# The second attention's scores and value products in fp32 instead of three fp32r products

## The reference, cut to what matters

```python
q = q * cos + _rotate_half(q) * sin          # 16 heads of 128, 256 tokens
kk = kk * cos + _rotate_half(kk) * sin       # 8 heads, each serves two query heads
att = jnp.einsum('shd,thd->hst', q, kk) / np.sqrt(HEAD_DIM)
att = jnp.where(causal[None], att, jnp.finfo(att.dtype).min)
att = jax.nn.softmax(att, axis=-1)
attn_out = jnp.einsum('hst,thd->shd', att, v).reshape(S, N_HEADS * HEAD_DIM) @ wo
x1 = x + attn_out
```

## Time and profile before

| | |
|---|---|
| median of 3 runs | 555.36 us (554.13 to 555.83) |
| profiled execution | 554.96 us |
| its span in the trace | 552.5 us |
| TensorE clock granted, mean | 0.976 of full speed |

### The profile page before, as it was taken

The page is one execution under the profiler, slowest core; times in us unless marked ns, Lnnn a source line. Parts: engine busy times, 40 slices in busy tenths (PEclk is TensorE's granted clock), DMA queues, the critical chain, the costliest instruction groups (busy, mean ns, idle before and its releaser), DMA issues. The chain is left out here.

```text
span 552.5 us, 11501 instructions
## 1 busy us (share of the span) xinstructions
PE 513.8 (93%) x4559; PEld 472.6 (86%) x4559; DVE 333.8 (60%) x647; ACT 256.0 (46%) x448; POOL 241.8 (44%) x207
## 2 busy tenths in 40 slices
PE   6978999999999999999998987889999799899984
PEld 6968899899999999989987976879988677799983
DVE  5977556763377887644437656899787545232331
ACT  8822233232256677422351426456767763554340
POOL 3022355242313432235257756544236124387983
PEclk9997999999999999999999988899999989999998
DMA  7813133202301011002405423545545632065522
GB/s 262 329 60 106 66 116 116 90 24 80 116 25 36 23 39 39 2 20 77 174 3 177 152 91 114 176 148 192 187 138 191 224 120 77 12 203 200 173 80 38
DMA packets 32884, 62.11 MB, mean 112 GB/s; under 512 B 3440, under 2 KB 3456, under 8 KB 32704
## 3 DMA queue, kind: packets, MB, share of 16 engines
q1 hardware_dynamic: 32288, 60.08, 32.5%
q0 software_dynamic: 544, 1.31, 1.2%
HBM read 48.27 MB, written 13.12 MB: 111 GB/s over the span
## 5 line engine op out<-in xcount | busy, mean ns | idle before, releaser
L1151 POOL TENSOR_TENSOR wlo<-raw,whi 128x512 fp32r<-128x512 f32 x96 | 129.7, 1383 | 106.3 <-ACT whi L525 106.2
L1215 PE MATMUL bank<-HTh,whi 128*128 128x256 f32 x224 | 64.6, 288 | 8.6 <-DVE rope L887 6.3
L1217 PE MATMUL bank<-HTh,wlo 128*128 128x256 f32 x224 | 64.1, 286 | 0.0
L1216 PE MATMUL bank<-HTl,whi 128*128 128x256 f32 x224 | 64.1, 286 | 0.0
L1132 POOL TENSOR_TENSOR state<-kv_new,state_dec 128x512 f32<-128x512 f32 x15 | 21.8, 1453 | 95.6 <-DVE kv_new L821 95.6
L810 DVE TENSOR_TENSOR A<-bank,DEC 128x512 f32<-128x512 f32 x64 | 39.7, 682 | 35.0 <-PE bank L1283 33.5
L525 ACT ACTIVATE whi<-raw 128x2048 fp32r<-128x2048 f32 x24 | 45.8, 1908 | 17.6 <-DMA raw<-in_w_down 12.5
L1215 PEld LDWEIGHTS bank<-HTh,whi 128*128 128x128 f32 x224 | 43.6, 195 | 10.0 <-issue 8.9
L1216 PEld LDWEIGHTS bank<-HTl,whi 128*128 128x128 f32 x224 | 43.6, 195 | 0.1
L1217 PEld LDWEIGHTS bank<-HTh,wlo 128*128 128x128 f32 x224 | 43.6, 195 | 0.0
L1261 PE MATMUL bank<-xTh,WKh 128*128 128x256 f32 x128 | 38.7, 303 | 2.3 <-DVE xTl L739 2.3
(11 more groups left out here) (283 smaller groups left out, 1560.1 us busy)
## 6 DMA issues: line engine op xcount, KB each, us to landing
X<-in_x SPq DMA_DIRECT2D x16, 256.0 KB, 3.4
xn_all<-XN SPq DMA_DIRECT2D x16, 256.0 KB, 2.8
uo_all<-uo SPq DMA_DIRECT2D x16, 256.0 KB, 2.7
raw<-in_wq SPq DMA_DIRECT2D x4, 1024.0 KB, 5.9
UR<-uo_all SPq DMA_DIRECT2D x16, 256.0 KB, 5.2
XR<-in_x SPq DMA_DIRECT2D x16, 256.0 KB, 3.0
out<-XR SPq DMA_DIRECT2D x16, 256.0 KB, 2.0
raw<-in_wo SPq DMA_DIRECT2D x4, 1024.0 KB, 5.9
```

The costliest lines, as they stand in the source:

```text
L1151: ins = Q.tensor_tensor(low[:, k, :], raw[b % 2][:, k, :], high[:, k, :].bitcast(f32), ALU.subtract)
L1215: T.matmul(dst, lh, rh, start=first, stop=False)
L1216: T.matmul(dst, lh, rl, start=False, stop=False)
L1217: return T.matmul(dst, ll, rh, start=False, stop=last)
```

## The change

The rotated queries and keys are written once, in fp32, straight into QR and KR by the sum that wrote `staged`. Values are copied once by ACT (VA). The transposed probabilities are copied once by ACT (PT). The low parts of queries, keys, values and probabilities are gone from DVE, and the high parts of queries and keys from ACT. The scores and the value product are one fp32 matmul each where there were three fp32r ones. The MLP's operand, which shared QRh and QRl, keeps its two parts under new names at the same addresses.

```diff
-        def unit_dst(u, part):
+        def unit_dst(u):
...
-                return (Vh, Vl)[part][i][:, p, :]
-            if k[0] == "Q":
-                return (QRh, QRl)[part][i][:, 2 * p:2 * p + 2, :].rearrange("p h m -> p (h m)")
-            return (KRh, KRl)[part][:, 4 * i + 2 * p:4 * i + 2 * p + 2, :].rearrange("p h m -> p (h m)")
+                return VA[i][:, p, :]
+            return QR[i][:, 2 * p:2 * p + 2, :] if k[0] == "Q" else KR[:, 4 * i + 2 * p:4 * i + 2 * p + 2, :]
...
-                    if u and units[u - 1][0][0] != "V":
-                        unit_high(u - 1)
-                    if units[u][0][0] == "V":
-                        unit_high(u)
+                elif u is not None and units[u][0][0] == "V":
+                    unit_values(u)
...
-                if h - 1 in unit_of_step:
-                    unit_high(unit_of_step[h - 1])
...
-                    S.activation(PTh[:, p % 2, :], B[4][:, 0:3 * P], ACT.Copy).then_inc(pt_hi, 1)
+                    S.activation(PT[:, p % 2, :], B[4][:, 0:3 * P], ACT.Copy).then_inc(pt_ok, 1)
...
-                if n >= 2:
-                    dve.wait_ge(unit_hi, before[-2] + 1), dve.wait_ge(unit_lo, before[-2] + 1)
...
-                V.tensor_tensor(staged[:, n % 2, :].rearrange("p (a m) -> p a m", a=2), rope1[:], rope2[:],
-                                ALU.add).then_inc(staged_ok, 1)
...
+                V.tensor_tensor(unit_dst(u), rope1[:], rope2[:], ALU.add).then_inc(rope_ok, 1)
...
-                if h - 1 in unit_of_step:
-                    unit_low(unit_of_step[h - 1])
...
-                if 0 <= p < FH:
-                    dve.wait_ge(pt_hi, p + 1)
-                    if p >= 2:
-                        dve.wait_ge(ot_ps, p - 1)
-                    low_of(PTl[:, p % 2, :], B[4][:, 0:3 * P], PTh[:, p % 2, :], pt_lo)
...
-                        pe.wait_ge(unit_lo, u + 1)
+                        pe.wait_ge(value_ok, value_count(u))
...
-                        ins = split_matmuls(B[h % 2][:, at:at + width],
-                                            (QRh[h // 4][:, h % 4, rows], QRl[h // 4][:, h % 4, rows]),
-                                            (KRh[:, kv, 0:width], KRl[:, kv, 0:width]), True, True)
+                        ins = T.matmul(B[h % 2][:, at:at + width], QR[h // 4][:, h % 4, rows], KR[:, kv, 0:width],
+                                       start=True, stop=True)
...
-                    pe.wait_ge(pn_ok, p + 1), pe.wait_ge(pt_lo, p), pe.wait_ge(ms_ok, N_TILES)
+                    pe.wait_ge(pn_ok, p + 1), pe.wait_ge(pt_ok, p), pe.wait_ge(ms_ok, N_TILES)
...
-                    split_matmuls(B[5][:, 0:SEL], (vh[:, 0, cols], vl[:, 0, cols]),
-                                  (PTh[:, g % 2, 0:SEL], PTl[:, g % 2, 0:SEL]), True, False)
-                    split_matmuls(B[5][:, P:SEL], (vh[:, 1, cols], vl[:, 1, cols]),
-                                  (PTh[:, g % 2, SEL:], PTl[:, g % 2, SEL:]), False, True).then_inc(ot_ps, 1)
+                    T.matmul(B[5][:, 0:SEL], VA[kv // 4][:, 0, cols], PT[:, g % 2, 0:SEL], start=True, stop=False)
+                    T.matmul(B[5][:, P:SEL], VA[kv // 4][:, 1, cols], PT[:, g % 2, SEL:], start=False, stop=True)\
+                        .then_inc(ot_ps, 1)
```

More of the change, by code:

```diff
@@ L59, in build @@
         xTh, xTl = (at(n, kb, [P, 2, NK, GROUP], f32r) for n, kb in (("xTh", 64), ("xTl", 72)))
-        KRh, KRl = (at(n, kb, [P, FKV, SEL], f32r) for n, kb in (("KRh", 64), ("KRl", 72)))
+        KR = at("KR", 64, [P, FKV, SEL])
         x1, delta = (at(n, kb, [P, NS, DM]) for n, kb in (("x1", 64), ("delta", 68)))
@@ L68, in build @@
         rope1, rope2 = (at(n, kb, [P, 2, SEL]) for n, kb in (("rope1", 88), ("rope2", 90)))
-        QRh, QRl = ([at(f"QR{i}{part}", kb, [P, 4, SEL], f32r) for i, kb in enumerate(homes)]
+        QR = [at(f"QR{i}", kb, [P, 4, SEL]) for i, kb in enumerate((112, 158, 96, 104))]
+        MTh, MTl = ([at(f"MT{i}{part}", kb, [P, 4, SEL], f32r) for i, kb in enumerate(homes)]
                     for part, homes in (("h", (112, 158, 96, 104)), ("l", (116, 162, 100, 108))))
         kh, kl, qh, ql = (at(n, 112 + 2 * i, [P, NK, P], f32r) for i, n in enumerate(("kh", "kl", "qh", "ql")))
-        Vh, Vl = ([at(f"V{i}{part}", kb, [P, NS, DM], f32r) for i, kb in enumerate(homes)]
-                  for part, homes in (("h", (92, 124)), ("l", (120, 128))))
+        VA = [at(f"VA{i}", kb, [P, NS, DM]) for i, kb in enumerate((92, 124))]
         X = at("X", 120, [P, NX, DM])
@@ L109, in build @@
         SM, PR, PN = (at(n, kb, [P, 2, 3 * P]) for n, kb in (("SM", 166), ("PR", 169), ("PN", 172)))
-        PTh, PTl = (at(n, kb, [P, 2, 3 * P], f32r) for n, kb in (("PTh", 175), ("PTl", 178)))
+        PT = at("PT", 175, [P, 2, 3 * P])
         OTh, OTl = (at(n, kb, [P, 2, SEL], f32r) for n, kb in (("OTh", 181), ("OTl", 183)))
@@ L204, in kq_count, with value_count @@
             return sum(units[n][0][0] != "V" for n in range(u + 1))
+        def value_count(u):
+            return u + 1 - kq_count(u)
         hi_after = {0: "Q2", 2: "O0", 4: "Q3", 6: "O1", 8: "O2", 9: "O3", 12: "G0", 16: "U0"}
@@ L282, in build @@
         cs_ok, ht_hi, ht_lo, sel_ok = sems("cs_ok ht_hi ht_lo sel_ok")
[L283 to L284 removed]
+        unit_ps, unit_b, rope_ok, value_ok = sems("unit_ps unit_b rope_ok value_ok")
+        sc_ps, sm_ok, exp_ok, pn_ok, pt_ps, pt_ok = sems("sc_ps sm_ok exp_ok pn_ok pt_ps pt_ok")
         sum_ok, ot_ps, ot_hi, ot_lo, wo_ps = sems("sum_ok ot_ps ot_hi ot_lo wo_ps")
@@ L537, in hidden_high, with unit_values @@
                         ins.then_inc(ht_hi, 1)
-            def unit_high(u):
-                if units[u][0][0] == "V":
[L541 to L546, removed]
+            def unit_values(u):
+                act.wait_ge(unit_ps, u + 1)
+                S.activation(unit_dst(u), job_bank("unit", u)[:], ACT.Copy).then_inc(value_ok, 1)
             def split_uo(N):
@@ L691, in _ @@
                     act.wait_ge(mt_ok, m + 1)
-                    S.activation(QRh[j][:, 2 * p:2 * p + 2, :].rearrange("p h m -> p (h m)"), staged[:, m % 2, :],
+                    S.activation(MTh[j][:, 2 * p:2 * p + 2, :].rearrange("p h m -> p (h m)"), staged[:, m % 2, :],
                                  ACT.Copy).then_inc(mt_hi, 1)
@@ L873, in stage @@
                 n = kq_count(u) - 1
-                before = [v for v in range(u) if units[v][0][0] != "V"]
-                if n >= 2:
-                    dve.wait_ge(unit_hi, before[-2] + 1), dve.wait_ge(unit_lo, before[-2] + 1)
                 dve.wait_ge(unit_ps, u + 1), dve.wait_ge(cs_ok, 1), dve.wait_ge(part_in, 16 * 5)
                 if n:
-                    dve.wait_ge(staged_ok, n)
+                    dve.wait_ge(rope_ok, n)
                 half = P // 2
@@ L904, in in_position @@
                 if u is not None:
[L905 to L910, removed]
+                    stage(u)
             def uo_low(N):
@@ L997, in _ @@
             for h in range(STEPS):
-                p, g = h - PT_AT, h - PV_AT
+                g = h - PV_AT
                 if h < FH:
@@ L1057, in _ @@
                     dve.wait_ge(mt_hi, m + 1)
-                    low_of(QRl[j][:, 2 * p:2 * p + 2, :], staged[:, m % 2, :].rearrange("p (a m) -> p a m", a=2),
-                           QRh[j][:, 2 * p:2 * p + 2, :], mt_lo)
+                    low_of(MTl[j][:, 2 * p:2 * p + 2, :], staged[:, m % 2, :].rearrange("p (a m) -> p a m", a=2),
+                           MTh[j][:, 2 * p:2 * p + 2, :], mt_lo)
             dve.wait_ge(ao_ok, 1)
@@ L1471, in _ @@
                     kv = h // (FH // FKV)
-                    pe.wait_ge(unit_lo, unit_needed(h)), pe.wait_ge(masked, 4 * N_TILES)
+                    pe.wait_ge(rope_ok, kq_count(unit_needed(h) - 1)), pe.wait_ge(masked, 4 * N_TILES)
                     if h >= 2:
@@ L1540, in down @@
                     for i in range(4):
-                        ins = split_matmuls(B[6 + t][:], (QRh[j][:, i, rows], QRl[j][:, i, rows]),
+                        ins = split_matmuls(B[6 + t][:], (MTh[j][:, i, rows], MTl[j][:, i, rows]),
                                             (high[:, i, :], low[:, i, :]), j == 0 and i == 0, j == 3 and i == 3)
```

7 lines of the change are left out of this document (2 added, 5 removed).

## The result

| | before | after |
|---|---|---|
| median | 555.6 us (554.13 to 556.56, 4 runs) | 539.5 us (538.16 to 542.64, 4 runs) |
| profiled execution, its span | 554.96, 552.5 us | 539.63, 537.8 us |
| mean granted clock of TensorE | 0.976 | 0.989 |

The ratio is 0.9723, with a 95% interval of 0.9696 to 0.9751: 16 us, or 2.8%, less. The forecast was 543.0 us, 12.0 less.

A forecast was written before the change was run, and what follows sets the result against it. DVE and ACT were taken to delay TensorE from chunk 15 to step 4, TensorE alone to set the pace afterwards. Sum: 554.96 - 9.5 - 3.0 - 0.5 + 1.0 = 543.0 us, range 538 to 550, likeliest 539 to 547.

The forecast's parts named there:

- Who bounds what: Chunk 15 to step 4: DVE and ACT late; afterwards TensorE alone sets the pace, a full step taking 8.72 us.
- Chunks 14 and 15: Before output 0: V1's unit starts 1.9 us earlier, half clock gives 1.7 us, output 0 at 336.0, 5.0 us ahead.
- Steps 0 to 4: First head loop steps: DVE's shorter steps bring unit 12 near 363.5; 9.5 us gained there, chunk 15's 5.0 included.
- rival (b): In steps 1 to 4, loads of UR take DVE's place, holding each by 1 us: 550.0 us, chance 0.12.
- fp32 products: Scores and value products of 16 heads: fp32 matmuls replacing fp32r ones cost 1.0 us more, bounds 0.8 to 2.4.
- the bound for the pair: One fp32 matmul of 128 and one of 256 columns, on TensorE, together cost 0.69 to 0.735 us.
- Rivals (c): Scores and value products pay four passes in full, by columns alone: 5.1 us instead of 1.0, 547.1 us, chance 0.07.
- (e): Scores and value products slower, by exposed weight loads or scores: 25.6 us more in all, 568.6 us, chance 0.06.
- The wait at 441.48: Before step 13's value product: less wait for OTl and half clock, 3.0 us gained, bounds 0 and 6.
- the tail: Last steps of the head loop: without PTl the chain is shorter, 0.5 us gained, bounds 0 to 1.
- After the loop: From the last wo product to the end, everything shifts whole, with the time between unchanged.
- Rival (d): No gain: POOL's block parts and their loads pace the steps, the lead lost by step 8: 555 us, chance 0.05.

The follow-up runs named there:

- experiments 3: The kernel after, with the unused split work of units 0 to 7 put back on ACT and DVE, no PTl: 545.68 us.
- Experiment 4: The kernel after, with only ACT's copies of rotated query and key units 0 to 7 put back, unused, no DVE low parts: 545.29 us.
- experiment 7: The kernel after, with the split work of units 8 to 15 and PTl (low part of the probabilities) put back, unused: 550.71 us.
- experiment 1: The kernel after, fp32 products kept, with all split work and its waits put back, its results unused: 558.52 us.
- experiment 9: The kernel before, with identity products filling TensorE's waits before V1's unit, output 0, step 13's value product and G0: 553.0 us.
- experiment 2: The kernel after, with each fp32 score and value product made three fp32r matmuls of the high parts, low parts left out: 541.34 us.
- 10: Experiment 1's kernel, with identity products filling the same four TensorE waits as in experiment 9: 551.02 us.
- experiments 5: The kernel after, with the split work of units 8 to 15 put back, unused, no PTl: 543.5 us.
- 6: The kernel after, with PTl (low part of the probabilities) put back on DVE for every head, unused, TensorE waiting for it: 544.63 us.
- Experiment 8: The kernel after, with identity products filling TensorE's waits before output 0 and before G0: 537.78 us.

## Why the prediction held, step by step

**Who bounds what.** DVE and ACT late in the first stretch, TensorE alone from step 4 to 12: right. The split work alone brings the waits back at the same places: those before V1's unit and output 0 in experiments 3 and 4, those of the head loop in experiment 7, all of them in experiment 1.

**Chunks 14 and 15**, foretold 319.0 and 336.0, came at 319.11 and 336.11, by the very chain: high part ahead of the rotation, then kv_new as the next thing late (1.15 us). The high part came 2.8 us sooner after unit 0, as counted in the forecast. Experiment 4 shows that it is ACT's place in line (4.7 us at output 0) and hardly DVE's subtraction (0.5).

**Steps 0 to 4**, term -9.5 for the first stretch with 8 to 10.5 as bounds, measured -10.8, outside them. Unit 9 came at 340.76 (341.0), unit 10 at 347.74 (347.7 to 348.1), unit 11 at 354.28 (355.3), unit 12 at 362.41 (363.1 to 364). My lists had DVE some 1 us too slow in step 2. They also left out half clock behind output 0 and unit 10 of the kernel before (windows of its trace):

```profile
342.00:343.00 1.00, 1.00 (x3) 0.75 (x3) 0.89 (x3) 0.77 (x4) 1.00 (x1) 0.50 0.68 221
...
356.00:357.00 1.00, 1.00 (x7) 1.00 (x6) 1.00 (x6) 0.62 (x4) 0.00 (x0) 0.50 0.60 209
```

Of the first stretch the clock has 3.0 us, by unit 12 in experiment 9; 1.7 were counted. A piece of rival (b) was there: uoh waited for UR in steps 2 and 3, DVE stood 1.86 us for it in step 3, and unit 12 waited 0.55. DVE's timeline of the kernel after:

```profile
357.93 1.39 DVE L858 TENSOR_TENSOR uol<-UR,uoh 128x512 fp32r<-128x512 f32 x1 [1.86 <-ACT uoh L551]
```

**fp32 products**, term +1.0 with 0.8 to 2.4 as bounds: wrong in sign. A full step takes 8.65 us (370.48 to 379.13) for 8.72, and one without a unit 5.77 for 5.86 (379.13 to 384.90, and 389.96 to 395.82 before). That is 0.07 to 0.09 less per head, 1.2 us in all. The step that failed is the bound for the pair, 0.69 to 0.735 us, and in it the 0.46 to 0.49 for a product of 256 columns, of which no row existed. That product takes 0.43 (377.09 to 377.52), and 4 x 256 columns at 2.4 GHz are 0.43. The pair takes 0.65 where no fp32r matmul follows closely (379.13 to the transposes at 379.78, 0.70 before), and 4 x 384 columns are 0.64. Where one follows, a part of the cost shows behind the pair: the value product takes 0.57 (377.09 to 377.66, 0.64 before) and wo 0.04 more (1.47 for 1.43); the scores take 0.46 (370.48 to 370.94), and with the unit behind them 3.53 (to 374.01) for 3.56. Experiments 2 (8.73 us for a full step with three fp32r products, 8.65 without) and 10 against 9 (2.0 less with fp32) agree in sign. By these rows the rule of four passes (the Trainium skill, FP8 and Floating Point Precision, TensorE Precision Notes) holds here. The error was to set it against three passes of fp32r: experiment 2's rows show that three of 128 columns take 0.29 us (371.15 to 371.44), where 384 columns at 2.4 GHz are 0.16, so that 4 to 3 in columns is no loss in time. Rivals (c) and (e) fall with it.

**The wait at 441.48 and the tail**, terms -3.0 and -0.5. From step 5's scores to the last three outputs (381.24 to 462.68 before, 370.48 to 446.47 after) 5.4 us were gained. fp32 has about 1.0 of them (0.07 to 0.09 for each of steps 5 to 12, and less in the rest), so the two terms came to -4.4. The wait itself gave 2.2 (3.01 to 0.83). The half clock behind it cost the value product, wo and the next scores of before 2.5 us (1.31, 2.66 and 1.29 us for 0.65, 1.46 and 0.65). Of that 1.05 went into waits for OTl in steps 14 to 17 (1.96 us after, 0.91 before). The faster clock brings them out: with the same split work and the clock kept, experiment 9 waits 0.75 in step 14, where the kernel before does not. A wait for UR remains at 421.16. That only 0.83 of the wait before step 13 are left because ACT comes to step 12 earlier against its load is argued, not shown; experiments 5 and 6 show how little slack there is (1.71 and 2.44).

**After the loop** everything shifts whole: right to G0 (16.2 at 462.68 and at 475.37), then 1.5 us are given back by half clock behind the wait of 2.29 us. The kernel before waits there too and kept its clock in its profiled execution. Experiment 8 fills the wait and gets 1.7 us. Without this stretch, which no term foresaw, the forecast would have been 4.9 us too high instead of 3.4: so much of its nearness is luck.

The sum with the sizes measured: 554.96 - 10.8 - 4.4 - 1.0 + 1.5 = 540.3, and the profiled execution has 539.63, since 0.6 us less lie around its span (2.46 before, 1.83 after). The forecast was 3.4 above that: 2.0 by the fp32 term, 1.3 by the first stretch, 0.9 by the wait and the tail, 0.6 around the span, less the 1.5 that the clock took at the end. Rival (d) falls with the lead that stayed. What came of the clock alone: 2.3 us of the kernel before by the medians of experiment 9, 3.8 in its trace. With TensorE kept busy in both, the kernels lie 15.2 us apart (553.0 and 537.8; 13.3 in the traces), so most of the gain is work and waits.

What stays open: why experiments 5 and 6 together bring 2 us more than their sum. Two parts are known: unit 12's wait, which comes back only with both, and half clock, of which the trace of experiment 7 has 3.4 us of full-clock time between 300 and 480 us and those of experiments 5 and 6 have 1.7 each, as much as the kernel after.

## What to carry to other kernels

Look at what stands behind a small instruction on its engine before looking at its duration: copies of 0.63 us on ACT, each waiting for DVE's rotation, held the next block's parts and cost 5 to 6 us, and DVE's subtractions beside them 0.5. When three short fp32r products can become one fp32 product, count the time per matmul in the trace and not the passes: at 128 and 256 columns fp32 was no dearer, and it needs no split operands. Price the clock behind TensorE's waits as well, but by a run: filled waits gave back about half of the lost 8.4 us in the kernel before, where other waits took up the rest, and all of 5.1 in experiment 1. Before two traces are laid side by side, look where the changed part starts in each.

## What the hardware showed that was not expected

- Half clock behind a wait does not come each time, and not by the wait's length. A wait of 2.3 us before G0 was followed by 0.59 over four us in the kernel after, and by full clock in the profiled execution of the kernel before. There 1.74 us before unit 10 were followed by half clock, 2.12 before unit 12 were not; in experiment 1 neither were 3.59 before output 0 and 3.10 in step 13. In experiment 2 half clock followed output 0's wait of 1.83, in the kernel after its 1.88 did not bring it. After the same wait of 2.6 us at V1's unit, that unit and the next took 7.29 us before and 8.46 in experiment 1, for 5.70 at full clock. The times of one kernel spread with the mean clock (experiment 1: 555.3 us at 0.981, 560.23 at 0.966).
- The 24 plain fp32 records of 128 columns ahead of output 0 in experiment 9 last 2.84 us together, the single record 0.28, so that they start every 0.11 us, a little under the 0.115 of the earlier trace rows's kdec.
- Three fp32r products of 128 columns cost 0.29 us (371.15 to 371.44 in experiment 2), one fp32 product of as many columns 0.22 (two such records) to 0.245.
